# Post-norm recurrent layer with a routed expert layer on eight cores: transposes of the scan regrouped, two waits removed, one load buffer doubled, one wait split

## The reference

```
xi = x @ Wi.T + bi
h[t] = tanh(xi[t] + h[t-1] @ Wh.T + bh)        # 2048 steps, one after the other
x  = layernorm(x + h)
route: top 4 of 16 experts by sigmoid(x @ gate_weight.T), in 2 of 4 groups
y  = sum over the experts of combine[t,e] * (silu(x @ gate[e].T) * (x @ up[e].T)) @ down[e].T
out = layernorm(x + y)
```

## Time and profile before

| what | us |
|---|---|
| median of 2 runs | 8522.67 |
| lowest and highest | 8515.7, 8529.65 |
| the profiled execution | 8396.73 |
| its span, slowest core (core 4) | 8395.1 |
| spans of the other cores | 8275.9 to 8392.1 |

### The profile page before, as it was taken

The page is one execution under the profiler, slowest core; times in us unless marked ns, Lnnn a source line. Parts: engine busy times, 40 slices in busy tenths (PEclk is TensorE's granted clock), DMA queues, the critical chain, the costliest instruction groups (busy, mean ns, idle before and its releaser), DMA issues. The chain is left out here.

```text
span 8395.1 us, 382533 instructions; the slowest of 8 cores (8275.9 to 8395.1 us)
## 1 busy us (share of the span) xinstructions
PE 6243.5 (74%) x170612; PEld 4580.9 (55%) x170612; DVE 1992.3 (24%) x9625; ACT 1282.3 (15%) x4381; POOL 44.2 (1%) x56
## 2 busy tenths in 40 slices
PE   5777777777777777777777777777774398988894
PEld 3666666666666666666666666666663133333331
DVE  1111111111111111111111111111114544444446
ACT  0111111111111111111111111111111000000000
POOL 0000000000000000000000000000000000000000
PEclk8555555665666566556555555556565599999996
DMA  2000000000000000000000000000001111112200
GB/s 45 4 4 4 4 4 4 4 4 4 4 4 4 4 4 4 4 4 4 4 4 4 4 4 4 4 4 4 4 4 42 30 31 31 31 31 34 42 16 40
DMA packets 51138, 100.71 MB, mean 12 GB/s; under 512 B 2919, under 2 KB 36200, under 8 KB 47482
## 3 DMA queue, kind: packets, MB, share of 16 engines
q0 software_dynamic: 45888, 58.76, 4.3%
q1 hardware_dynamic: 3642, 17.48, 0.6%
HBM read 126.59 MB, written 8.39 MB: 16 GB/s over the span
## 5 line engine op out<-in xcount | busy, mean ns | idle before, releaser
L209 PE MATMUL zB<-whT,hstat 128*32 128x128 f16 x65536 | 2584.9, 295 | 37.8 <-issue 35.7
L209 PE MATMUL zA<-whT,hstat 128*32 128x128 f16 x65536 | 2547.0, 292 | 81.6 <-issue 60.5
L209 PEld LDWEIGHTS zB<-whT,hstat 128*32 128x32 f16 x65536 | 1919.5, 139 | 64.5 <-issue 59.7
L209 PEld LDWEIGHTS zA<-whT,hstat 128*32 128x32 f16 x65536 | 1760.6, 134 | 193.3 <-issue 185.5
L198 PE MATMUL zA<-xi_stream,id_sb 128*32 128x128 f16 x8192 | 602.7, 273 | 1045.5 <-DVE buf_h L184 1033.5
L253 ACT ACTIVATE hsp<-zA 128x128 f16<-128x128 f32 x2048 | 568.5, 278 | 4905.9 <-PE zA L209 4905.9
L183 DVE CAST hstat<-tpA 128x4 f16<-128x4 f32 x2048 | 333.6, 163 | 3776.6 <-PE tpA L220 3776.6
L198 PEld LDWEIGHTS zA<-xi_stream,id_sb 128*32 128x32 f16 x8192 | 288.0, 99 | 1171.3 <-issue 1170.5
L220 PEld LDWEIGHTS tpA<-sel_sb,hsp 128*32 128x32 f16 x8192 | 285.3, 99 | 864.2 <-issue 863.7
L220 PE MATMUL tpA<-sel_sb,hsp 128*32 128x4 f16 x8192 | 405.5, 179 | 416.6 <-ACT hsp L253 364.5
L187 DVE CAST hstat<-tpB 128x4 f16<-128x4 f32 x2048 | 333.1, 163 | 1548.6 <-PE tpB L220 1548.6
(11 more groups left out here) (119 smaller groups left out, 2161.4 us busy)
## 6 DMA issues: line engine op xcount, KB each, us to landing
wg<-gpT POOLq DMA_DIRECT2D x16, 1024.0 KB, 9.0
wu<-upT POOLq DMA_DIRECT2D x16, 1024.0 KB, 13.4
wd<-dpT POOLq DMA_DIRECT2D x16, 1024.0 KB, 18.0
xbuf<-x_fm SPq DMA_DIRECT2D x8, 1024.0 KB, 5.0
outT<-och SPq DMA_DIRECT2D x8, 1024.0 KB, 3.9
x<-x_fm POOLq DMA_DIRECT2D x1, 4096.0 KB, 33.3
wiT<-wiT POOLq DMA_DIRECT2D x1, 2048.0 KB, 45.1
whT<-whT POOLq DMA_DIRECT2D x1, 2048.0 KB, 55.3
```

The costliest lines, as they stand in the source:

```text
L209: mi = te.matmul(out=zb_[par][32 * g:32 * g + 32, 0:128], lhsT=bass.AP(hstat, par * 8 + COLOF(kc), [[16, 128], [0, 32]]), rhs=whT16[:, kc ...
```

## The change

Four things change.

- Scan, TensorE: the transposes tpB of step t go behind tpA of the same step, after a wait for th1, and no longer behind seed B of step t+1. The waits at the head of a step are th1 of step t-2 (from the third step on) and ev; the wait for th1 between the seeds is gone.
- Scan, ScalarE: each tanh waits for its matmuls alone; the waits for tr and tr1 are gone.
- First layer norm: xbuf is two chunks long, loads go to its halves in turn, on a semaphore of their own each, and a load waits for VectorE's addition of the chunk two before it.
- Experts, TensorE: of the eight groups of down matmuls only the first waits for act16, and there each matmul waits for its own slice.

```diff
+        s_ld3b = sem("ld3b")
...
-                        te.wait_ge(s_th, t)
-                        te.wait_ge(s_ev, t + 1)
-                        xi_seed(t, zA, 0)
-                        te.wait_ge(s_th1, t)
-                        xi_seed(t, zB, 128)
-                        if t >= 1:
-                            transp(t - 1, tpB, 128, s_tr1)
...
+                        if t >= 2:
+                            te.wait_ge(s_th1, t - 1)
+                        te.wait_ge(s_ev, t + 1)
...
                         te.wait_ge(s_th, t + 1)
-                        transp(t, tpA, 0, s_tr)
-                    te.wait_ge(s_th1, t_steps)
-                    transp(t_steps - 1, tpB, 128, s_tr1)
...
+                        ti.then_inc(s_tr, 1)
+                        te.wait_ge(s_th1, t + 1)
+                        for j in range(4):
+                            ti = te.matmul(out=tpB[par][32 * j:32 * j + 32, 0:4],
...
                         sc.wait_ge(s_mm, t + 1)
-                        if t >= 2:
-                            sc.wait_ge(s_tr, t - 1)
...
                         sc.wait_ge(s_mm1, t + 1)
-                        if t >= 2:
-                            sc.wait_ge(s_tr1, t - 1)
...
-            xbuf = p3.enter_context(nc.sbuf_tensor("xbuf", [128, T], F32))
+            xbuf = p3.enter_context(nc.sbuf_tensor("xbuf", [128, 2 * T], F32))
...
-                    if cc >= 1:
-                        sync.wait_ge(s_dv3, 3 * cc - 2)
-                    sync.dma_start(out=xbuf[:, :], in_=x_fm[128 * cc:128 * (cc + 1), :]).then_inc(s_ld3, 16)
+                    if cc >= 2:
+                        sync.wait_ge(s_dv3, 3 * (cc - 1) - 2)
+                    sync.dma_start(out=xbuf[:, (cc % 2) * T:(cc % 2) * T + T],
+                                   in_=x_fm[128 * cc:128 * (cc + 1), :]).then_inc(
+                                       s_ld3 if cc % 2 == 0 else s_ld3b, 16)
...
-                                te.wait_ge(s_dvm, 2 * (base_q + 4))
                                 if gidx >= 2:
                                     te.wait_ge(s_dev, gidx - 1)
                                 for kci in range(4):
+                                    if hc == 0:
+                                        te.wait_ge(s_dvm, 2 * (base_q + kci + 1))
```

More of the change, by code:

```diff
@@ L192, in _ @@
                 def _(te):
-                    def xi_seed(t, zb_, ofs):
+                    halves = [(zA, 0), (zB, 128)]
+                    for t in range(t_steps):
+                        par = t % 2
                         blkofs = (t // 128) * D
                         r = t % 128
[L196 to L207, removed]
-                            for g in range(4):
[L209 to L214, removed]
+                        if t >= 2:
+                            te.wait_ge(s_th1, t - 1)
@@ new lines, in _ @@
+                        te.wait_ge(s_ev, t + 1)
+                        for zb_, ofs in halves:
+                            for g in range(4):
+                                te.matmul(out=zb_[par][32 * g:32 * g + 32, 0:128],
+                                          lhsT=bass.AP(id_sb, r, [[128, 128], [0, 32]]),
+                                          rhs=xi_stream[:, blkofs + 256 * g + ofs: blkofs + 256 * g + ofs + 128],
+                                          start=True, stop=False, tile_position=(0, 32 * g),
+                                          skip_group_check=True)
@@ new lines, in _ @@
+                        for zb_, ofs in halves:
+                            for kc in range(0, KC, 2):
+                                for g in range(4):
+                                    te.matmul(out=zb_[par][32 * g:32 * g + 32, 0:128],
+                                              lhsT=bass.AP(hstat, par * 8 + COLOF(kc), [[16, 128], [0, 32]]),
+                                              rhs=whT16[:, kc * D + 256 * g + ofs: kc * D + 256 * g + ofs + 128],
+                                              start=False, stop=False, tile_position=(0, 32 * g),
+                                              skip_group_check=True)
@@ new lines, in _ @@
+                        te.wait_ge(s_ev1, t + 1)
+                        for zb_, ofs, s_done in [(zA, 0, s_mm), (zB, 128, s_mm1)]:
+                            for kc in range(1, KC, 2):
+                                for g in range(4):
+                                    mi = te.matmul(out=zb_[par][32 * g:32 * g + 32, 0:128],
+                                                   lhsT=bass.AP(hstat, par * 8 + COLOF(kc), [[16, 128], [0, 32]]),
+                                                   rhs=whT16[:, kc * D + 256 * g + ofs: kc * D + 256 * g + ofs + 128],
+                                                   start=False, stop=(kc == KC - 1), tile_position=(0, 32 * g),
+                                                   skip_group_check=True)
@@ L215, in z_rounds @@
                             mi.then_inc(s_done, 1)
-                    def transp(t, tp_, hofs, s_done):
-                        par = t % 2
+                        te.wait_ge(s_th, t + 1)
                         for j in range(4):
-                            ti = te.matmul(out=tp_[par][32 * j:32 * j + 32, 0:4],
-                                           lhsT=hsp[:, par * 256 + hofs + 32 * j: par * 256 + hofs + 32 * j + 32],
+                            ti = te.matmul(out=tpA[par][32 * j:32 * j + 32, 0:4],
+                                           lhsT=hsp[:, par * 256 + 32 * j: par * 256 + 32 * j + 32],
@@ L243, in _ @@
[L243 to L244 removed]
+                        ti.then_inc(s_tr, 1)
+                        te.wait_ge(s_th1, t + 1)
+                        for j in range(4):
+                            ti = te.matmul(out=tpB[par][32 * j:32 * j + 32, 0:4],
+                                           lhsT=hsp[:, par * 256 + 128 + 32 * j: par * 256 + 128 + 32 * j + 32],
+                                           rhs=sel_sb[:, :], start=True, stop=True,
+                                           tile_position=(0, 32 * j))
@@ L375, in pre3 @@
             def pre3(v, cc, dvc):
-                v.wait_ge(s_ld3, 16 * (cc + 1))
+                if cc % 2 == 0:
+                    v.wait_ge(s_ld3, 16 * (cc // 2 + 1))
+                else:
+                    v.wait_ge(s_ld3b, 16 * (cc // 2 + 1))
                 v.wait_ge(s_dv3, dvc)
-                v.tensor_tensor(out=buf_u[:, cc * T:(cc + 1) * T], in0=xbuf[:, :],
+                sl_x = slice((cc % 2) * T, (cc % 2) * T + T)
+                v.tensor_tensor(out=buf_u[:, cc * T:(cc + 1) * T], in0=xbuf[:, sl_x],
                                 in1=buf_h[:, cc * T:(cc + 1) * T], op=OP.add).then_inc(s_dv3, 1)
```

11 lines of the change are left out of this document (1 added, 10 removed).

## The result

The changed kernel takes 8134.57 us (median of 11 runs) against 8519.22 (10 runs): ratio 0.9505, 95% interval 0.9415 to 0.9594. The direction was right and the size was half of it.

What follows compares the result with a forecast made beforehand. It took the scan to be bound by its chain of dependent work from tanh to tanh, plus instruction stalls. Terms -61 - 60 - 35 - 45 - 9 = -210 us gave 8313 us, range 8150 to 8470.

Steps and rivals of the forecast that it cites:

- term C: Scan: TensorE gets busier, so its granted clock rises by 0.015, -35 us (ends 0 and -230).
- the clock climbs: Rival, scan: clock rises by 0.10 and all gains from shorter steps stay, -505 us, 8018 us; chance 0.12.
- the supply: Scan: TensorE's instructions arriving late, put at 300 us of stalls, 0.15 us a step, in some 40% of steps.
- kept part of A and B: Scan: after stalls, 60% of the ScalarE wait gain (-61 us) and half of the tpB gain (-60 us) stay.
- term B: Scan, TensorE: moving tpB behind tpA gains 0.34 us a step at 2.4 GHz, 119 us, and nothing at 1.2 GHz.
- Term A: Scan, ScalarE: dropping the waits on tr and tr1 saves 0.05 us a step, at most 102 us.
- the ring: Scan step's path: tanh of zA, transpose tpA, VectorE's two copies, seeds, zA matmuls, next tanh; 3.00 us at 1.2 GHz.
- 300 us of unexplained time: Scan: 6294 us taken against 5994 us computed from step times at both clocks; the rest was called instruction stalls.
- the supply is no bound: Rival, scan: stalls are tied to places and do not grow, gains kept whole, -310 us, 8213 us; chance 0.15.
- The slack for tpB: Scan, TensorE: tpB comes 0.85 us after the tanh, seeds due at 1.11, leaving 0.15 us at 1.2 GHz; no cost.
- the slower rival: Scan: early tpB delays the seeds to 1.20 us, +0.09 us a step, +184 us, 8653 us; chance 0.04.
- Terms D and E: Behind the scan: shorter act wait in the experts, -45 us, and double xbuf in the first layer norm, -9 us.

Runs made afterwards that it cites:

- e1_act: Kernel before with only ScalarE's waits on tr and tr1 taken out; ratio 0.9886 to the kernel before.
- e2_tpb: Kernel before with tpB moved behind tpA and the wait for th1 between the seeds gone, ScalarE's second waits kept; ratio 0.973.
- e5_bfill: Kernel before plus two unused 256-column matmuls a step in TensorE's idle stretches; ratio 0.9776 to the kernel before.
- e6_afill: Changed kernel plus two unused 256-column matmuls a step in TensorE's idle stretches; ratio 0.9512 to the kernel before.
- e3_th1: Kernel before with only the wait for th1 moved from between the seeds to the head of the step; ratio 0.9958.
- e8_tp1: Changed kernel with each group of four transposes made one matmul, 153 instead of 165 TensorE instructions a step; ratio 0.9145 to the kernel before.
- e9_more: Changed kernel plus 12 tiny unused matmuls a step, 189 instead of 165 TensorE instructions; ratio 1.0255 to the kernel before.
- e4_rest: Kernel before with only the layer norm and experts changes, scan as before; ratio 0.9956 to the kernel before.
- e10_whole: Changed kernel with 256-column seeds and rounds, single transposes and early seeds, 80 TensorE instructions a step; ratio 1.0062 to the kernel before.

## Why the forecast was wrong, and where it was right

**The step that failed is term C, the clock.** I took +0.015 and -35 us for it; the scan's clock rose by 0.094, and that is worth some 210 us. By the estimate below the price was about right, 22 us per 0.01 where I had 23; the size was not. In the table a fifth of the steps with one level ran at 2.4 GHz before (345 of 1684 a core), and nearly half after (683 of 1444). With the shares of before, the means of the changed kernel give 0.8 x 3.066 + 0.2 x 2.635 = 2.980 us against 3.056, 0.076 less; with its own shares 2.863, another 0.117. Put to the 344 us that the scan lost, that is, as an estimate, some 135 us for shorter steps (the forecast had 121 for A and B) and some 210 us for the clock. e1_act shows it by itself: with a ring shorter by 0.055 us the clock rose by 0.08, and in e2_tpb by 0.045. By what way the change reaches the clock stays open. e5_bfill and e6_afill show that two matmuls of 256 columns more in each step raise it; in e3_th1 the steps were shorter too, and the clock fell. I had the mechanism as a rival, "the clock climbs", with 0.12 and +0.10 of clock. It came in that size, but with the supply's stalls on top, which that rival left out, so its 8018 us was too low. The chance was too small for the one case that had the clock right. The range should have reached to where both hold: all of its clock and the forecast's kept part of A and B is -61 - 60 - 230 - 54 = -405 us. The profiled executions lie 403.5 us apart (8396.73 and 7993.18), but the clock was taken at its end there and term B at 1.2 GHz at nothing, so the nearness is in part luck.

**Term A** was right in size: 0.055 us on the ring (e1_act).

**Term B** was right at 2.4 GHz (0.337 against 0.34 in e2_tpb) and wrong at 1.2 GHz. I read two paces of 0.105 and 0.108 us per group as "no gap"; the run holds 0.045 (e2_tpb), of which 0.018 are the wait's place (e3_th1). That is the second step that failed, and it was in every step at 1.2 GHz. The six groups of the earlier trace rows had a gap after the zA seeds and then closer starts, and an average over them can't show what the run would be without either. The rule of the Trainium skill ("TensorE: Matmul & The Clock Gate", section "Wait — 56ns, not 53.3ns?") would have had 0.1 us for four tiny matmuls, an estimate; measured are 0.027 at 1.2 GHz. In the trace of the changed kernel the four matmuls of tpB, each on its own 32 columns of the array, start 3 to 4 ns apart (from 1023.21 us on).

**What is kept.** The supply takes a part of what the ring gives: at 1.2 GHz the shortest step fell by 0.100 and the mean by 0.060, at 2.4 GHz by 0.391 and 0.141. So 60% and 36% were kept, where the forecast had 60% and half. As an estimate from 300 us of unexplained time this held, and the place of the gaps, e8_tp1 and e9_more show that its cause was the right one. One sum in it was off: 16% of 6294 us are 1007 us and make 392 steps of 2.57 us, not 350. The table has 20% of the steps before at 2.4 GHz. The rival "the supply is no bound" is out, and with it the words of the Trainium skill ("Runtime: NRT & Kernel Launch", Instruction fetch mechanics) that a block's crossing is mostly hidden: in this scan the stalls are 0.1 to 0.7 us a step. The blocks of 256 instructions that the Trainium skill has in that section agree with the packets.

**Cover.** The slack for tpB ahead of the seeds held (0.84 and 1.11 us, as forecast), so the slower rival had no ground. **Terms D and E:** 57 us (e4_rest) against 54.

## What to carry to other kernels

A recurrence is bound by its ring, but what the ring's links cost depends on the clock. A small cut on the ring can be worth more than its length (e1_act: 173 us of the scan, where the cut itself is 113), though it need not (e3_th1), and one unused matmul a step was worth more than either. When the shortest step and the mean step differ, look where in the queue the gaps stand: if it is the same place of every block of 256 instructions, it is the supply of instructions, and wider matmuls, even on a longer ring, are the way out. Removing one of the two bounds alone can show nothing (e6_afill 0.951, as the changed kernel; e10_whole 1.006); both together gave 0.794.

## What the runs showed of the hardware

- In this unrolled scan TensorE's instructions come in blocks of 256, and the gaps inside a run of matmuls stand where a block ends (all of 490 to 515 gaps on each core of the changed kernel). The mean over a scan was 4.31 to 4.73 us for 256 instructions in eleven variants at clocks of 0.58 to 0.96. With 80 instructions a step no such gap is left.
- A second semaphore wait that is long met costs 0.055 us on ScalarE (e1_act).
- The granted clock of a recurrence can change much with a small part of a step: e1_act, with a step of 2.949 us for 3.004, had 0.682 for 0.605, and e3_th1, with 2.986, had 0.582. A run of 256-column rounds with nothing behind it had 0.500, and with one unused matmul of 256 columns 0.928.
- Matmuls that write unused columns of an idle accumulator in TensorE's idle time cost nothing on the ring at 2.4 GHz (2.568 and 2.177 with and without).
